# New orders for the engines, and a rebuilt end around the scan, in a one-core Trainium2 kernel

## What is computed

```
x = L0(x, ctx, mask)    # 16-head self-attention on layer_norm(x) with the mask, + ctx @ Wg, then a ReLU feed-forward (1024)
x = L1(ctx, x)          # cross-attention on the normed ctx (values cut to 4 columns), GELU, self-attention of the result
x = L2(x, ctx)          # 16-head causal attention on ctx, GELU feed-forward (1024)
x = L3(x, ctx, program) # 8-head attention on ctx, then a state-space scan:

U = (layer_norm(x) @ W_in.T + b_in) @ Bmat             # 16 batches x 128 steps x 64 states
def step(s, u_t):
    s = silu(s @ A.T) + u_t
    return (s, s)
_, states = jax.lax.scan(step, zeros, U.transpose(1, 0, 2))
out = x + einsum('tbs,sh->bth', states, Cmat) + (program.mean(axis=1) @ W_prog.T + b_prog)
```

## Time and profile before

| | us |
|---|---|
| median of 3 runs | 904.4 (901.54 to 906.85) |
| profiled execution, its own time | 900.69 |
| its span, first to last instruction | 898.5 |
| PE busy | 752.9 (84%) |
| DVE / ACT / POOL busy | 538.7 / 428.9 / 336.6 |
| mean granted clock of PE | 0.913 of full |

### The profile page before, as it was taken

How to read it: one execution, slowest core, us unless ns; L and a number is a source line. 1 busy time by engine, 2 the same in 40 slices (tenths; PEclk the granted TensorE clock), 3 DMA queues, 4 the chain that set the end, 5 groups by cost and what they waited for, 6 DMA issues and landing times.

```text
span 898.5 us, 16236 instructions
## 1 busy us (share of the span) xinstructions
PE 752.9 (84%) x5488; PEld 608.1 (68%) x5488; DVE 538.7 (60%) x2244; ACT 428.9 (48%) x1760; POOL 336.6 (37%) x343
## 2 busy tenths in 40 slices
PE   0799897799799979997999899979899787575556
PEld 0587676688678858886888688867787576344445
DVE  1558578647847884788478948884876572310003
ACT  0735265565553855385538554781464451312221
POOL 3224263434534552454345533652345251100000
PEclk9899899999999999999999999999999899555556
DMA  8500000100000000000000000000000000010002
GB/s 318 202 7 19 24 13 7 26 1 1 19 1 24 1 19 1 24 1 19 1 24 2 13 1 25 1 1 2 1 1 1 1 2 0 1 24 0 1 0 94
DMA packets 15861, 20.83 MB, mean 23 GB/s; under 512 B 3613, under 2 KB 12322, under 8 KB 15138
## 3 DMA queue, kind: packets, MB, share of 16 engines
q1 hardware_dynamic: 15778, 19.79, 6.7%
...
## 4 chain that ended last, share of the span: by engine, by line
PE 66%; DVE 18%; ACT 5%; issue 5%; POOL 3%; DMA 2%; SPq 1%; DVEq 0%; POOLq 0%
PE work_bank L572 21%; PE work_bank L563 20%; PE scores_bank L771 6%; PE work_bank L701 5%; DVE probsT L1012 4%; DVE probs L911 4%; PE work_bank L555 3%; PE work_bank L621 3%; ACT probs L1153 3%; PE scores_bank L599 2%; DVE xn L929 2%; ACT probs L1090 2%; DVE stats L948 2%; POOL probs L794 1%; DMA bias<-in_mask 1%
## 5 line engine op out<-in xcount | busy, mean ns | idle before, releaser
L794 POOL TENSOR_TENSOR probs<-probs,rtotal 128x512 f32<-128x512 f32 x160 | 164.7, 1042 | 217.9 <-DVE rtotal L1002 217.6
L1090 ACT ACTIVATE probs<-probs,nmx 128x128 f32<-128x128 f32 x512 | 197.9, 390 | 78.8 <-DVE nmx L911 78.4
L1012 DVE COPY probsT<-work_bank 128x512 f32<-128x512 f32 x160 | 106.5, 680 | 16.6 <-PE work_bank L701 16.6
L701 PE MATMUL work_bank<-ident,probs 128*128 128x128 f32 x640 | 97.5, 292 | 21.4 <-POOL probs L794 14.7
L572 PE MATMUL work_bank<-L_w,hidden 128*128 128x256 f32 x512 | 113.9, 380 | 0.0
L572 PEld LDWEIGHTS work_bank<-L_w,hidden 128*128 128x128 f32 x512 | 96.0, 190 | 14.1 <-ACT hidden L1145 1.7
L794 POOL TENSOR_TENSOR rstd<-veps,half 128x2 f32<-128x2 f32 x64 | 45.5, 712 | 158.1 <-DVE veps L956 157.7
L701 PEld LDWEIGHTS work_bank<-ident,probs 128*128 128x128 f32 x640 | 76.4, 149 | 41.4 <-POOL probs L794 22.0
L1090 ACT ACTIVATION_READ_ACCUMULATOR probs<-probs,nmx 128x1 f32 x512 | 97.1, 190 | 0.0
L771 PE MATMUL scores_bank<-probs,a_t 64*64 64x16 f32 x252 | 49.5, 275 | 33.4 <-ACT probs L1153 33.4
L555 PE MATMUL work_bank<-ident,xn 128*128 128x128 f32 x256 | 42.2, 288 | 35.1 <-DVE xn L929 35.1
...
## 6 DMA issues: line engine op xcount, KB each, us to landing
...
```

The costliest lines, as they stand in the source:

```text
L701: mm = nc.tensor.transpose(d[:, j * P:j * P + P], src[:, j, :], ident[:])
L794: return nc.gpsimd.tensor_tensor(out, a0, a1, op)
L1012: nc.vector.tensor_copy(turn_slot(s, i, key), d[:].rearrange("p (j k) -> p j k", j=4))\
L1090: ins = nc.scalar.activation(e_at[slot][:, j, :], src, ACT.Exp, bias=nmx[:, slot, j:j + 1], scale=1.0 if s == "C" else -1.0, accum_out=tot ...
```

## The change

Four things change together.

1. All five order tables are new. The number of steps is the same. The first two roots stand before `A0.xb` on POOL, and the masks' conversions (`bias`) stand later on DVE.
2. `prog` becomes the last of `REST_LOADS` and lands in a part of `x7_all` that is free then; its 16 mean products run at `B0.score.0` beside `drive_weight`, on another bank half.
3. `occupy` issues products that nothing reads: 32 columns of weights by 128 (or 144) moving columns. They stand on PE ahead of the steps of the last `C` stage and after each of the first 66 steps of the scan.
4. The seeding of `s_bank` 1 to 3 moves between scan steps 8, 40 and 72. The final products for positions 0 to 63 and 64 to 95 are cut into 64 pieces, of which 60 stand one behind each scan step from 67 (and 100) on; those of positions 96 to 127 follow the scan as 16 products of 32 columns, on rows that four DMAs have gathered in `late`. The first SiLU (on zeros) moves ahead of the last `drive`. The output is stored in 16 + 4 DMAs, two of them from ACT.

```
 LOAD_ORDER = """
-mask.1 x.1 c.1 t.1 mask.2 mask.3 x.2 c.2 t.2 x.3 mask.4 c.3 t.3 x.4 mask.5 c.4 t.4 x.5 mask.6 c.5 t.5 x.6 mask.7 c.6
-t.6 x.7 c.7 t.7
+mask.1 c.1 x.1 t.1 mask.2 t.2 x.2 mask.3 c.2 x.3 t.3 c.3 mask.4 x.4 t.4 c.4 mask.5 x.5 t.5 c.5 mask.6
+x.6 t.6 c.6 mask.7 x.7 t.7 c.7
...
+OCCUPIED = {("C", NT - 1, ("flip", "x6")): 14, ("C", NT - 1, ("q",)): 3, ("C", NT - 1, ("turn", 0)): 14,
+            ("C", NT - 1, ("turn", 1)): 2, ("C", NT - 1, ("turn", 2)): 2, ("C", NT - 1, ("turn", 3)): 2,
+            ("C", NT - 1, ("mix",)): 2, ("C", NT - 1, ("out",)): 2, ("C", NT - 1, ("flip", "x7")): 14,
+            ("C", NT - 1, ("drive",)): 4}
...
+            def occupy(d, n, columns=P):
+
+                for _ in range(n):
+                    nc.tensor.matmul(d[0:32, 0:columns], wq["L0"][:, 0, 0:32], wk["L0"][:, 0, 0:columns], start=True,
+                                     stop=True, skip_group_check=True)
...
+            ready(exped, EXPED["C", NT - 1, ("exp", 3)])
+            occupy(s_bank[3], 4)
+            pe.wait_ge(*done("C", NT - 1, "drive"))
+            mm = from_u(0)
+            part = 0
             for t in range(1, P):
-                if t == 2:
-                    for w in range(W_BANKS):
-                        pe.wait_ge(drained[w], len(range(w, len(FILLS), W_BANKS)))
-                    pe.wait_ge(prog_loaded, 16)
-                    for b in range(B):
-                        means_mm = nc.tensor.matmul(w_bank[3][SS:P, b:b + 1], prog[:, b, :], mean_w[:], start=True,
-                                                    stop=True)
-                    means_mm.then_inc(prog_meant, 1)
                 if t > 1:
                     pe.wait_ge(silued, t - 1)
                     mm = nc.tensor.matmul(s_bank[t // 32][0:SS, (t % 32) * B:(t % 32) * B + B], a_t[:],
                                           w_state[:, t - 1, :], start=False, stop=True, skip_group_check=True)
                 mm.then_inc(stepped, 1)
...
+                if t in (8, 40, 72):
+                    from_u(t // 32 + 1)
+                elif t < FIRST_FROM:
+                    occupy(s_bank[3], 1, P + 16)
+                if t >= (FIRST_FROM if part < 2 * B else SECOND_FROM) and t != 72:
+                    last_part(part)
+                    part += 1
+
+            pe.wait_ge(states_ready, 5)
+            for g in range(4):
+                for j in range(4):
+                    mm = nc.tensor.matmul(s_bank[g // 2][32 * j:32 * j + 32, (g % 2) * D:(g % 2) * D + D],
+                                          stT[:, 4 * g + j, FIRST + SECOND:P], w_last[:], start=True, stop=True)
+                if g % 2:
+                    mm.then_inc(late_filled, 1)
+            for k in range(part, 4 * B):
+                last_part(k)
```

More of the change, by code:

```diff
@@ new lines @@
+A4.flip.x2 G4.v1 B3.q A4.ffn1.2 B3.score.0 A4.ffn1.0 A4.ffn1.3 A4.ffn1.1 B3.score.1 B3.turn.0 B3.turn.1 A4.ffn2
+B3.turn.2 B3.turn.3 B3.turn.4 B3.turn.5 C2.out B3.mix.0 B3.turn.6 B3.turn.7 J4.k B3.mix.1 M4.flip.x3 H5.q B3.flip.o
+C2.flip.x7 M4.score.a A5.score.0 K3.v J4.v B3.flip.x5 C2.drive B3.ffn1.0 B3.ffn1.2 B3.ffn1.1 B3.ffn1.3 M4.turn.a
+A5.turn.0 A5.turn.1 A5.score.1 B3.ffn2 M4.mix.a A5.turn.2 A5.turn.3 A5.turn.4 M4.cross C3.flip.x6 A5.mix.0 A5.turn.5
+C3.q A5.turn.6 A5.turn.7 H6.flip.x C3.score A5.mix.1 M4.flip.cr H6.v M4.score.s A5.out K4.k C3.turn.0 C3.turn.1
@@ L89 @@
+C6.flip.x6 B7.q C6.q B7.score.0 B7.score.1 B7.turn.0 B7.turn.1 C6.score B7.turn.2 K7.k B7.turn.3 B7.turn.4 B7.mix.0
+B7.turn.5 B7.turn.6 B7.turn.7 C6.turn.0 B7.mix.1 B7.flip.o C6.turn.1 C6.turn.2 C6.turn.3 B7.flip.x5 C6.mix B7.ffn1.0
+B7.ffn1.2 B7.ffn1.1 B7.ffn1.3 C6.out B7.ffn2 C6.flip.x7 K7.v C6.drive C7.flip.x6 C7.q C7.score C7.turn.0 C7.turn.1
+C7.turn.2 C7.turn.3 C7.mix C7.out C7.flip.x7 C7.drive
 """
@@ L162 @@
[L162 to L163 removed]
+A0.max.4 A0.max.5 A0.turn.1 A0.turn.0 A0.rec.3 A0.max.6 A0.max.7 G1.bias A0.rec.2 A0.rec.4 H1.stat.x A0.rec.5
+A0.turn.2 A0.turn.3 A0.rec.6 G2.bias A0.rec.7 H1.norm.x A0.turn.4 A0.mix.0 A0.turn.5 A0.turn.6 A0.turn.7 H1.flip.x
+A0.mix.1 H1.v A0.out A0.stat.x2 J0.v A0.norm.x2 A0.flip.x2 A1.max.0 A1.max.1 A1.max.2 A0.ffn1.2 A1.max.3 A1.rec.1
+A0.ffn1.0 A1.rec.0 A0.ffn1.3 A1.rec.2 A0.ffn1.1 A1.turn.1 A1.rec.3 A1.turn.0 A1.turn.2 A0.ffn2 A1.turn.3 M0.stat.x3
@@ new lines @@
+B1.stat.x5 C0.flip.x7 B1.norm.x5 A3.max.0 A3.max.1 A3.max.2 B1.flip.x5 C0.drive J2.v A3.rec.1 M2.rec.a A3.max.3
+A3.rec.0 A3.rec.2 H4.norm.x G3.stat.c A3.rec.3 G3.norm.c M2.turn.a A3.turn.0 A3.turn.1 A3.max.4 A3.max.5 A3.max.6
+A3.max.7 A3.rec.4 A3.rec.5 B1.ffn2 A3.rec.6 C1.stat.x6 A3.turn.4 A3.rec.7 A3.turn.2 C1.norm.x6 A3.turn.3 G5.bias
+C1.flip.x6 M2.stat.cr A3.turn.5 A3.mix.0 A3.turn.6 A3.turn.7 M2.norm.cr H4.flip.x C1.max.0 M2.flip.cr A3.mix.1
+C1.max.1 H4.v M2.max.s C1.max.2 C1.max.3 C1.rec.0 C1.rec.1 C1.rec.2 A3.out M2.rec.s A3.stat.x2 C1.rec.3 C1.turn.0
@@ L645, in drive_weight @@
                                           start=(k == 0), stop=(k == DC - 1))
+                for b in range(B):
+                    mm = nc.tensor.matmul(d[SS:P, 2 * P + b:2 * P + b + 1], prog[:, b, :], mean_w[:], start=True, stop=True)
                 mm.then_inc(set_up_pe, 1)
@@ new lines, in _ @@
+            states(0, 32)
+            states(32, FIRST)
+            for n in range(NT - 1):
+                add_last(n)
+            states(FIRST, FIRST + SECOND)
+            before_end = (P - SECOND_FROM) // 4
+            for n in range(NT - 1, NT + before_end - 1):
+                add_last(n)
+            states(FIRST + SECOND, P - 1)
+            states(P - 1, P)
+            add_last(NT + before_end - 1)
+            for k in range(2):
+                add_late(k)
+            for n in range(NT + before_end, 2 * NT):
+                add_last(n)
@@ L1154, in _ @@
                     .then_inc(silued, 1)
+            for j in (2, 3):
+                act.wait_ge(late_added, 2)
+                nc.scalar.dma_start(out[:, FIRST + SECOND:P].rearrange("(g j) s d -> j s g d", j=4)[j],
+                                    late[32 * j:32 * j + 32]).then_inc(out_stored, 16)
 def _columns(inputs):
```

416 lines of the change are left out of this document (210 added, 206 removed).

## The result

The changed kernel takes 874.2 us in the median of 4 runs (873.15 to 874.46), the kernel before in the same comparison 903.1: a ratio of 0.968 (95% interval 0.965 to 0.971), so faster by 29 us. 852 was predicted, with 836 to 872 as the range. The profiled execution took 873.15 us (span 871.4) where before it took 900.69 (898.5).

A forecast was written before the change was run, and what follows sets the result against it. PE, over 90% busy, was taken to bound the main part, and a serial chain with PE at 1.2 GHz the rest from 755 us. Terms summed to -50.5 us: 900.7 to 850.2, predicted as 852, range 836 to 872.

The forecast's parts named there:

- The roots first: Start: first roots run right away, PE's first transpose 9.7 us earlier; -8.0 us, bounds -9.7 and -4.
- The masks later: Main part: later conversions remove DVE's waits for mask loads, four of six on the chain; -9.2 us, bounds 0 and -12.3.
- The rest of the tables: Main part: same steps otherwise ordered, no row prices a new order; taken as 0, bounds -12 and +8.
- The means: Sixteen mean products at B0.score.0 at full clock plus DVE's extra copy; +1.9 us, bounds +1 and +3.5.
- The last C stage: Last C stage: unread products hold the full clock, halving the time of chain work; -8.0 us, bounds -8.5 and +5.
- Seeding: Before the scan: one seeding and one SiLU left of 10.46 us; -8.9 us.
- The scan: 126 scan steps at full clock, 0.54 us instead of 0.66, -15.0 us; three seedings inside it, +1.4 us.
- The end: After the last SiLU: 7.9 us instead of 12.6; -4.7 us, bounds -6 and -2.
- The clock's rival: C stage, seeding and scan: unread products fail to hold the clock, giving 890 us; chance 0.12.

The follow-up runs named there:

- e6: Changed kernel with the conversions of masks 3, 5, 6 and 7 moved back behind the last maximum of the pair two before; 872.5 us, ratio 0.965.
- e10: Changed kernel with POOL's A0.xb back at the head of its order, ahead of the first roots; 882.9 us, ratio 0.978.
- e18: New end with old order tables (only A0.xb behind the first roots), prog loaded later, unread products ahead of 11 main-part steps; 867.1 us, ratio 0.961.
- e1: Kernel before with only the five new order tables, keeping its old end; 903.9 us, ratio 0.999.
- e16: Changed kernel plus later prog load, start steps reordered on DVE and POOL, and sized unread products ahead of main-part steps; 853.1 us, ratio 0.943.
- e7: Changed kernel with prog's load moved behind the second pair's loads, with its own semaphore; 872.6 us, ratio 0.963.
- e8: Changed kernel with A0.rec.2 earlier and mask 1's conversion later on DVE, and A0.nrm.2 ahead of A0.nrm.3 on POOL; 872.0 us, ratio 0.963.
- e2: Changed kernel with the five old order tables, so only the new end; 876.8 us, ratio 0.969.
- e3: Changed kernel without any unread product, the last stage's pieces staying between scan steps; 910.7 us, ratio 1.007.

## Why the prediction was wrong

It missed by 22 us. By its terms -50.5 was forecast and the span fell by 27.1: 18.8 us are missing in the main part (-15.3 forecast, +3.5 found), 4.6 behind it (-35.2 forecast, -30.6 found). Two steps of the prediction failed: it took the masks' waits for 9.2 us of path, which e6 does not find, and it put the rest of the new tables at 0, while waits that they move let the clock fall and cost more than they save.

- **The roots first, -8.0.** Right: 8.7 by e10.
- **The masks later, -9.2.** This step failed. I put the wait's full length on the path because the chain of waits names it four times, two of them in the earlier trace rows, and a period with it is 2.9 us longer. Putting it back in the new orders cost nothing (e6), so the bound of 0 is the value found there, and not for the reason given: DVE did wait again, and PE's period stayed the same. Two periods of the old table differ in more than their waits. Whether the waits cost something in the old orders was not tried; in e18 they stand on the chain even with the clock held.
- **The rest of the tables, 0.** This step failed as well. Orders alone are worth 0 (e1), roots -8.7 and masks 0, so by difference the rest costs 8.7, with some 3 us of uncertainty from e1's interval, where at most +8 was allowed. By the marks: up to `B1` the 9.7 us of the first transpose shrink to 1.3, though by e10 the roots' share is still whole there; `B1` to `B5` is won, 350.9 to 341.3 us; from `B5` to `C7` 150.8 become 165.1. I looked at waits, not at what they do to the clock. The mean granted clock of the three stretches shown above is 0.92, 0.98 and 0.90; that of the kernel before stands behind this list: 0.96, 1.00 and 0.97. In the changed kernel PE stands 1.26 us in 265 to 270 us, then has 0.66 of the clock for 5 us at full work, and so in each period. Waits of 3 to 6 us at the start and in the drain do the same. e16 takes most of the falls away (mean granted clock 0.994, against 0.953) and 21 us with them, of which e7 and e8 account for some 3; the other 18 are about what the main part missed. By the Trainium skill ("TensorE: Matmul & The Clock Gate", section "HAM oscillation — how this bites in real kernels") TensorE's waits for DMA, repeated from tile to tile, let the clock fall each time, so that the next tile starts slow. The traces here agree for waits of 3 to 6 us, though these are for VectorE and GpSimd; the fall in the steady period comes after much shorter ones, 0.79 us the longest.
- **The means, +1.9.** Too small: `C7`'s product moves 3.4 us from e1 to the changed kernel; of this 2.0 is the load's place (e7). With the old tables the new end costs 8.2 us in the main part (e2); most of it stands at `B1` already, and its cause stays open.
- **The last C stage, -8.0.** -7.1: from `C7`'s query product to the seeding 31.75 us before, 24.64 now.
- **Seeding, -8.9.** -9.1: 10.46 to 1.34 us.
- **The scan, -15.0 and +1.4.** -9.9 instead of -13.6: 83.1 to 73.2 us. The mechanism was right, the step mis-sized: 0.575 and 0.55 us instead of 0.54, some 3 us over 126 steps. The two weight loads take 0.19 us where at half clock they took 0.28, PE's part 0.28 instead of 0.39, the way to and from ACT is the same, and beside the 144 columns a step waits another 0.025 us.
- **The end, -4.7.** -4.4: 8.2 us.
- **The clock's rival** was priced at 890 us. e3 shows that losing it costs more, 910.7, since pieces put 0.22 us on a step.

Busy time of the kernel before in the same three stretches of the main part:

```profile
22.00:258.00 236.00, 205.47 (x1506) 169.52 (x1510) 160.48 (x734) 126.05 (x495) 93.61 (x94) 0.96 0.10 31
258.00:600.00 342.00, 318.77 (x2536) 262.86 (x2536) 255.61 (x1094) 198.72 (x829) 164.95 (x164) 1.00 0.03 11
600.00:755.00 155.00, 139.82 (x1018) 114.43 (x1018) 93.44 (x346) 72.27 (x273) 61.26 (x61) 0.97 0.00 1
```

From 600 to 755 us PE worked 139.8 us there and works 131.2 now, at a lower clock: both make that stretch longer.
